# Routing of a mixture-of-experts stage, moved into the drain of the scan before it

## The reference, cut to what matters

```
h = layernorm(x) * (1 + ca) + sa
x = x + ga * scan_layer(h)            # in_proj, conv, selective scan, out_proj
h = layernorm(x) * (1 + cb) + sb      # [8192 tokens, 256]
s = h @ Wg                            # 8 logits a token
routed = softmax(s[:, :7]); keep only the largest, divided by itself
shared = softmax(s[:, 7:])            # one expert that every token passes
y = sum over experts e of gate_e * ((silu(h @ W1b_e) * (h @ W1a_e)) @ W2_e)
out = x + gb * y
```

## Time and profile before

| | us |
|---|---|
| median of 3 runs (lowest, highest) | 2514.27 (2513.76, 2518.05) |
| the profiled execution, its own time | 2508.63 |
| its span, first to last instruction | 2506.6 |
| PE busy in the span | 2176.9 (87%) |
| DVE busy | 1929.8 (77%) |
| POOL busy | 1955.7 (78%) |
| ACT busy | 1360.7 (54%) |

### The profile page before, as it was taken

The page is one execution under the profiler, slowest core; times in us unless marked ns, Lnnn a source line. Parts: engine busy times, 40 slices in busy tenths (PEclk is TensorE's granted clock), DMA queues, the critical chain, the costliest instruction groups (busy, mean ns, idle before and its releaser), DMA issues. The chain is left out here.

```text
span 2506.6 us, 31126 instructions
## 1 busy us (share of the span) xinstructions
PE 2176.9 (87%) x7664; PEld 1058.5 (42%) x7665; DVE 1929.8 (77%) x2060; ACT 1360.7 (54%) x2440; POOL 1955.7 (78%) x840
## 2 busy tenths in 40 slices
PE   8769898988989898999898898989857649999997
PEld 3214343443434343434343443434323335566654
DVE  2799999999999999989999999999897162222222
ACT  3666666667575766666666667576644232222221
POOL 1999889898989898988989898989897014555553
PEclk9868989898989898988989898989878869999999
DMA  5443242424232333424242424232321062222221
GB/s 154 135 110 94 76 103 67 101 68 113 81 92 74 96 82 87 116 79 105 68 103 69 101 68 111 81 94 77 89 68 42 24 208 76 85 84 83 87 85 45
DMA packets 149401, 224.39 MB, mean 90 GB/s; under 512 B 48227, under 2 KB 85617, under 8 KB 145138
## 3 DMA queue, kind: packets, MB, share of 16 engines
q1 hardware_dynamic: 135858, 182.44, 28.0%
q0 software_dynamic: 13376, 40.12, 5.2%
HBM read 99.48 MB, written 31.47 MB: 52 GB/s over the span
## 5 line engine op out<-in xcount | busy, mean ns | idle before, releaser
L1023 POOL TENSOR_TENSOR hs<-hs,c_rep 128x2048 f32<-128x2048 f32 x256 | 1154.5, 4528 | 37.3 <-ACT state L767 37.2
L863 DVE TENSOR_TENSOR_SCAN hs<-dA,state,hs 128x512 f32<-128x512 f32 x768 | 931.1, 1264 | 21.0 <-ACT dA L747 16.7
L747 ACT ACTIVATE dA<-d_rep,a 128x512 f32<-128x512 f32 x1024 | 690.0, 686 | 427.7 <-DVE hs L863 423.2
L1016 POOL TENSOR_TENSOR hs<-u_rep,b_rep 128x2048 f32<-128x2048 f32 x96 | 435.5, 4536 | 88.9 <-PE bank L517 88.9
L850 DVE TENSOR_TENSOR hs<-u_ps,b_rep 128x2048 f32<-128x2048 f32 x160 | 360.9, 2272 | 8.0 <-issue 4.8
L488 PE MATMUL bank<-n,w1s 128*128 128x512 f32 x512 | 268.4, 661 | 68.0 <-DVE delta L831 39.2
L863 DVE TENSOR_TENSOR_SCAN hs<-dA,hs 128x512 f32<-128x512 f32 x256 | 294.0, 1202 | 19.7 <-ACT dA L747 18.6
L517 PE MATMUL bank<-hs,spread 128*32 128x512 f32 x2048 | 280.3, 696 | 32.1 <-POOL hs L1023 28.0
L1408 DVE TENSOR_TENSOR hid<-z,sg 128x512 f32<-128x512 f32 x70 | 48.4, 692 | 298.1 <-ACT sg L1386 298.1
L1326 PE MATMUL z<-w1r,hT 128*128 x560 | 260.5, 608 | 3.4 <-issue 2.4
L446 PE MATMUL bank<-xin,w_in 128*128 128x512 f32 x512 | 245.1, 619 | 9.2 <-ACT xin L600 9.2
(11 more groups left out here) (173 smaller groups left out, 2531.9 us busy)
## 6 DMA issues: line engine op xcount, KB each, us to landing
d_rep<-delta SPq DMA_DIRECT2D x1024, 64.0 KB, 2.0
u_rep<-us SPq DMA_DIRECT2D x384, 64.0 KB, 2.0
b_rep<-bc_rows SPq DMA_DIRECT2D x64, 256.0 KB, 4.7
c_rep<-bc_rows SPq DMA_DIRECT2D x64, 256.0 KB, 7.8
xres<-in_x SPq DMA_DIRECT2D x16, 512.0 KB, 3.6
token_rows<-xpad SPq DMA_DIRECT2D x32, 256.0 KB, 2.3
token_rows<-xres SPq DMA_DIRECT2D x16, 512.0 KB, 3.0
xin<-in_x SPq DMA_DIRECT2D x15, 512.0 KB, 9.5
```

The lines of the kernel that those rows point to most:

```text
L747: nc.scalar.activation(dA[:, u % ABANK, :], d_rep[:, q, :], ACT.Exp, scale=t["a"][:, u:u + 1]).then_inc(da_ready, 1)
L863: nc.vector.tensor_tensor_scan(hs[:, s % RING, g, :], dA[:, u % ABANK, :], hs[:, s % RING, g, :], state[:, u:u + 1] if m else 0.0, ALU.mul ...
L1016: nc.gpsimd.tensor_tensor(hs[:, s % RING], u_rep[:, i % UBUF, :].unsqueeze(1).to_broadcast([P, NG, T]), b_rep[:, par, :].rearrange("p (g t ...
L1023: nc.gpsimd.tensor_tensor(hs[:, s % RING, :, :], hs[:, s % RING, :, :], c_rep[:, par, :].rearrange("p (g t) -> p g t", g=NG), ALU.mult).th ...
```

## The change

The routing program goes; its work moves into the drain of the fused program, in two parts, and its barrier goes with it. Part one (index 0) is tiles 0 to 59, whose logits are in memory when body 15 ends; part two (index 1) is the last chunk's four tiles, read from `lg` directly, whose logits are no longer stored. All tables live in memory that the drain no longer uses (`Room` hands it out: first weights, `us`, `delta`, spreads); sums and `placed` in PSUM banks of the scan.

Slot tiles are no longer sorted by expert. Each expert's running count starts at 127; where it crosses a multiple of 128 the next free slot tile goes to that expert (`allot`, `hand_out`), so tiles are numbered in order of arrival and part one's are final without knowing part two. `settle` computes each token's slot. The expert's number is packed above the token number (`pack`) and goes through the same matmul, from which `owner` is read at the end. The gate half of `sel`, ACT's before, and the number half, DVE's before, are now one POOL multiplication (`weigh_slots`), in groups with two alternating buffers. PE gets `count` and `place` between its items, and ACT two exponentials.

SP loads the expert weights during the drain, `w2r` as soon as the last scan products are made and `w1r` after the last `SUM`, into the memory of the scan's ring and of `b_rep` and `c_rep`, right behind the `XR` load. In the experts program the gate rows get a semaphore of their own, so that the first transposes wait for the token rows only, and in body 0 PE does `z` of tile 0 ahead of turning tile 1.

The core of the diff, shortened:

```diff
+            hold(sp, logits_stored, 16 * (NCHUNK - 1), held)
+            sp.dma_start(early_logits, logits_dram[0:EARLY_TILES * P]...).then_inc(early_loaded, 16)
+            def load_routed():
+                hold(sp, hc_ready, NSET * NCHUNK, held)
+                sp.wait_ge(dbu_own, N_OWN * NCHUNK)
+                sp.wait_ge(dbu_shared, N_SHARED * NCHUNK)
+                for e in range(NR):
+                    sp.dma_start(t["w2r"][:, e], ...).then_inc(w_routed, 16)
+                hold(sp, y_ready, KI * NCHUNK, held)
+                for e in range(NR):
+                    sp.dma_start(t["w1r"][:, e], ...).then_inc(w_routed, 16)
             for c in (NCHUNK, NCHUNK + 1):
                 for kind, n in transfers:
                     ...
                         transfer(kind, n, c, c % CPB)
+                        if kind == "XR":
+                            load_routed()
...
+            def count(i):
+                r = parts[i]
+                pe.wait_ge(onehot, i + 1)
+                if i == 0:
+                    pe.wait_ge(consts, 11)
+                nc.tensor.matmul(flat(r.total), ones, flat(r.one), start=True, stop=True).then_inc(counted, 1)
+                nc.tensor.matmul(flat(r.prefix), below, flat(r.one), start=True, stop=True).then_inc(counted, 1)
+            def place(g):
+                pe.wait_ge(id_ready, g + 1)
+                pe.wait_ge(lane_ready, g + 1)
+                for n, j in enumerate(groups[g]):
+                    last = nc.tensor.matmul(placed, at_lane[:, g % 2, n, :], sel[:, g % 2, n, :], ...)
+                last.then_inc(placed_made, 1)
+            PLACES = {("OP", 0): [(count, 0)], ("B", 2): [(count, 1)], ("A", 0): [(place, 0), (place, 1)], ("A", 1): [(place, 2)],
+                      ("A", 2): [(place, 3)], ("A", 3): [(place, 4)], ("Y", 0): [(place, 5), (place, 6)]}
...
+            route_exp(0)
             for item in [...]:
                     do(item, NCHUNK, 0)
+                    if item[0] == ("B", 0):
+                        route_exp(1)
...
+            def spread_slots(g):
+                dve.wait_ge(slots_known, 1 + g // len(EARLY_GROUPS))
+                if g >= 2:
+                    dve.wait_ge(placed_made, g - 1)
+                v.tensor_tensor(at_tile[:, g % 2, 0:n], among(kidx, SLOT_TILES), spread(r.tile, SLOT_TILES), ALU.is_equal).then_inc(at_ready, 1)
+                v.tensor_tensor(at_lane[:, g % 2, 0:n], among(lanes, P), spread(r.lane, P), ALU.is_equal).then_inc(lane_ready, 1)
+            FIRST, LAST = 0, 1
+            ROUTED = {("Y", 1): [(choose, FIRST)], ("SUM", 3): [(pick, FIRST)], ("OP", 0): [(allot, FIRST)],
+                      ("LN2", 0): [(hand_out, FIRST), (settle, FIRST), (weigh, FIRST), (spread_slots, 0), (soften, LAST), (spread_slots, 1),
+                                   (choose, LAST), (pick, LAST), (weigh, LAST), (allot, LAST), (hand_out, LAST), (settle, LAST)],
+                      ("A", 0): [(spread_slots, 2)], ("A", 1): [(spread_slots, 3)], ("A", 2): [(spread_slots, 4)],
+                      ("A", 3): [(spread_slots, 5), (spread_slots, 6)], ("Y", 0): [(spread_slots, 7)]}
+            soften(FIRST)
             for c in (NCHUNK, NCHUNK + 1):
                 ...
                         do(item, c, c % CPB)
+                        if c == NCHUNK:
+                            for step, n in ROUTED.get(item[0], []):
+                                step(n)
+            spread_slots(len(groups) - 1)
...
+            def weigh_slots(g):                                   # POOL, after its own last items
+                hold(pool, at_ready, g + 1, held)
+                if g >= 2:
+                    pool.wait_ge(placed_made, g - 1)
+                nc.gpsimd.tensor_tensor(sel[:, g % 2, 0:n]..., at_tile[:, g % 2, 0:n]..., r.value[:, first:first + n]..., ALU.mult).then_inc(id_ready, 1)
...
-                pe.wait_ge(fetched[q], 32 * n + 32)
+                pe.wait_ge(fetched[q], 16 * n + 16)
...
+                if first(k, 1):
+                    expert_in(k, q)
                 if not is_last(k, 1):
                     turn(*at(1))
                 if not first(k, 1):
                     turn_hid(*at(-1)[:2])
-                expert_in(k, q)
+                    expert_in(k, q)
```

More of the change, by code:

```diff
@@ L15 @@
+import math
 from contextlib import ExitStack
@@ L55 @@
 EMPTY = 1 << 20
+GR = 8
+EARLY_TILES = NTILE - TT
+EARLY_GROUPS = [range(g, min(g + GR, EARLY_TILES)) for g in range(0, EARLY_TILES, GR)]
+PACK = BATCH * SEQ * 2
 def hold(eng, sem, value, held):
@@ L62, in hold, with __init__, take @@
     eng.sem_inc(held, 1)
+class Room:
+    def __init__(self, *parts):
+        self.parts = [[part, 0] for part in parts]
+    def take(self, shape, dt=F32):
+        size = math.prod(shape)
+        for part in self.parts:
+            if part[1] + size <= part[0].shape[1]:
+                x = part[0][:, part[1]:part[1] + size]
+                part[1] += size
+                x = x if dt == F32 else x.bitcast(dt)
+                names = "abc"[:len(shape)]
+                return x.rearrange("p (" + " ".join(names) + ") -> p " + " ".join(names), **dict(zip(names, shape))) if len(shape) > 1 else x
+        raise ValueError("no room")
+class Routing:
+    def __init__(self, take, n, logits, keep_e, keep_w, total, prefix):
+        self.n, self.w, self.logits, self.keep_e, self.keep_w, self.total, self.prefix = n, n + 1, logits, keep_e, keep_w, total, prefix
+        self.ex, self.pr, self.mask, self.cum, self.work = (take([n, NR]) for _ in range(5))
+        self.one = take([NR, n])
+        self.tot, self.incl, self.nt, self.hd, self.nn, self.held = (take([NR, n + 1]) for _ in range(6))
+        self.ii = take([NR, n + 1], I32)
+        self.new, self.alloc = take([n, NR]), take([n, NR])
+        self.mx, self.rs, self.pm, self.ss, self.slot, self.tile, self.lane = (take([n]) for _ in range(7))
+        self.value = take([n, 2])
+        self.posi, self.lanei = take([n], I32), take([n], I32)
 def fused_program(nc, ins, t, bc_dram, wout_dram, w2_dram, mod_dram, gb_dram, rows_dram, logits_dram):
@@ L366, in transfer @@
                     store_rows(c - 1)
-                elif kind == "LOG":
+                elif kind == "LOG" and not (known(c) and c == NCHUNK):
                     store_logits(c - 1)
@@ L581, in _ @@
                         group(g, off, c, c % 2)
+                        if off == -1 and c == NCHUNK:
+                            for step, n in PLACES.get(g, []):
+                                step(n)
+            place(7)
+            pe.wait_ge(id_ready, len(groups))
+            pe.wait_ge(lane_ready, len(groups))
+            for n, j in enumerate(groups[-1]):
+                last = nc.tensor.matmul(placed, at_lane[:, (len(groups) - 1) % 2, n, :], sel[:, (len(groups) - 1) % 2, n, :], start=False, stop=(j == NTILE - 1))
+            last.then_inc(all_placed, 1)
         @block.scalar
@@ L1239, in experts_program @@
+            for g in range(len(groups)):
+                weigh_slots(g)
 def experts_program(nc, t, rows_dram, gb_dram, out):
@@ L1435, in build @@
             fused_program(nc, ins, t, bc_dram, wout_dram, w2_dram, mod_dram, gb_dram, rows_dram, logits_dram)
[L1436 to L1441 removed]
+        experts_program(nc, keep, rows_dram, gb_dram, out)
 def laid_out(x):
```

320 lines of the change are left out of this document (171 added, 149 removed).

## The result

The kernel after takes **2471.86 us** (median of 4 runs, 2468.68 to 2473.09) against 2514.02 for the kernel before in the same comparison (4 runs, 2513.11 to 2518.05). The ratio is 0.9827, 95% interval 0.981 to 0.9844. The direction was right, the size was not.

A forecast was written before the change was run, and what follows sets the result against it. PE bounds the routed experts, so whatever starts them earlier is gained whole: 27.5 us up to POOL's first copy plus 2.2 at the expert start, 29.7; 2478.9 plus 5.6 carried over gives 2484.6 us, range 2474 to 2494.

The forecast's parts named there:

- The weights are hidden: Drain: 11.0 MB of expert weights start at 1941 and are in by 1980.5, hidden by 40 us.
- rival B: Drain: the weight loads hold back `xres`, which `OP0` needs; 2489.5 us at half price, chance 0.10.
- Turns between DVE and POOL: Drain: POOL's `weigh_slots` holds part two's subtraction 2.4 us and `choose(1)`'s multiplication 2.2; `onehot` comes at 1978.2.
- The tail of routing: After the last accumulation: last spread, POOL, `place` and DVE steps take 5.8 us, then a barrier of 0.5.
- The expert start: Filling of the expert pipeline: first `z` 6.0 us behind POOL's first copy, second at 16.1 against 18.3; gain 2.2.
- rival D: Routed experts: slot tiles in arrival order change the expert at most tiles; at 0.5 us a tile 2519.6, chance 0.03.
- The 5.6 us carried from the profiled execution to the median: Whole kernel: median of runs 2514.27 lies 5.6 us above the profiled 2508.63; added to 2478.9.
- From `A0` to the last accumulation: End of drain: 28.5 us of PE work in one queue; 30.1 us from first read against 19.9 now, +10.2.
- The added wait on PE: Drain: `count(1)` waits 4.9 us for part two's `onehot`, with `B3` and `A0` queued behind; `A0` 7.7 later, clock included.
- the clock: Drain: PE's gap ahead of `count(1)` is followed by a granted clock of 0.50, +1.7 us.
- The normalisation: Drain: `count(0)` on PE makes `OP1` 0.65 us late, and the normalisation and all behind it 0.65 late.
- Rival A: Drain: no turns between DVE and POOL, no clock drop; gain 39.1 us, 2475.2, chance 0.18.

The follow-up runs named there:

- experiment 4: Kernel after with the expert weights loaded behind the drain, after SP's waits for `ACC` and `ROWS`: 2500.27 us, ratio 0.9957.
- experiment 3: Kernel after with POOL's first two `weigh_slots` held back until part two's slots are known: 2476.69 us, ratio 0.9860.
- experiment 2: Kernel after with the two edits in the experts program taken back: 2479.32 us, ratio 0.9868.
- experiment 11: Kernel before, unchanged, profiled once more: one run, 2514.66 us.
- experiment 1: Kernel before with only the experts program's two edits (gate rows' own semaphore, first `z` ahead of tile 1's transposes): 2504.56 us, ratio 0.9965.
- experiment 5: Kernel before with only the gate rows' own semaphore: one run, 2506.01 us.
- experiment 6: Kernel before with only the first `z` ahead of tile 1's transposes, gate and token rows on one semaphore: one run, 2518.53 us.
- experiment 9: Kernel before with DVE's wait on `fetched` written twice: one run, 2510.1 us.
- experiment 10: Kernel before with the gate rows' own semaphore, but PE waiting for both semaphores: one run, 2508.65 us.
- experiment 7: Kernel after with each `place` matmul of the first 60 tiles issued twice, the copy into unused PSUM: median 2477.15 us, ratio 0.9861.

## Why the prediction was wrong in size, step by step

Right:
- *The weights are hidden, at no cost* (experiment 4), and `xres` is not held back: in the kernel after `OP0` is read at 1951.91, straight after PE's result. That is rival B gone.
- *Turns between DVE and POOL*, from the one row: both appeared, at the two places named, and vanish in experiment 3. There were more places than forecast (below). The Trainium skill, "SBUF — State Buffer", section "Who interferes with whom", lets reductions through, which no row of before showed; here it agrees: the reduction at 1979.53 takes 0.17 beside POOL's multiplication, the two-input instruction 0.4 us later 1.63.
- *The tail of routing*: 6.4 from the last accumulation to the copy, forecast 6.2.
- *The expert start*: first `z` at 6.0 as forecast. The second at 15.8 against 16.1 is partly luck, since it moves by over 1 us with the clock.
- *The order of slot tiles costs nothing a tile* (rival D): 415.3 us over the tiles against 415.6, and 415.3 again in experiment 2, whose experts program is that of before.
- *The 5.6 us carried from the profiled execution to the median*: experiment 11 shows that execution to have had an early scan end.

Wrong, in the order of size:
- **The end of the kernel, 5.2 us, missing from the sum.** "Expert start" priced the semaphore split for the first tile only. Experiments 1, 2, 5, 6, 9 and 10 tie the 5.2 to it. Nothing in the profile before would have given this number; but the 12.0 us between the last store and the end were there to be asked about.
- **"From `A0` to the last accumulation", 30.1 forecast, 26.7 measured.** The bound was the one named (experiment 7); the size of its work was not. "28.5 us in one queue" added recorded durations: 3 x 2.0, 2 x 3.7, 7 x 2.15. Counted from start to start, as the profile after and experiment 7 show them, the same work is 3 x 1.71 + 2 x 3.45 + 7 x 1.91 = 25.4. Nor does that whole queue lie behind the first read: `place(0)` and `(1)` began at 1986.54, right behind `A0`'s multiplication and 3.1 us ahead of DVE's read. The forecast's steps from one read to the next were 4.2, 5.1, 4.4, 7.2 and 8.5; measured are 3.6, 4.8, 3.7, 6.5 and 7.3. In them lie three `A`, five `place` groups and two `Y`, so durations in place of distances make 3 x 0.29 + 5 x 0.24 + 2 x 0.25 = 2.6 of the 3.4; the other 0.8 are not split further. The profile before had the distance for `B`, the shape of `A`: ACT's copies of it begin 1.71 us apart (1971.30, 1973.01, 1974.73).
- **"The added wait on PE" and "the clock", 2.6 us together.** `count(1)` waited 1.04 instead of 4.9, and no clock drop followed. `onehot(1)` came at +45.1 (forecast +46.6): the turns cost 3.1 instead of 4.6, because POOL's multiplication needs 2.0 us alone (two took 4.08 in experiment 3), not 2.57, which I had scaled from another shape. And PE's `B2` ended at +44.1, 2.5 later than in before instead of 0.65, so that the gap shrank from the other side too (2.1 of it is the next point; and the clock was 0.50 in the first 3.65 us of `B`, where before had 0.65). The first `A` was read at +52.2 (forecast +54.8), and now DVE's own list set it: it ends 0.8 behind SiLU. The forecast's own terms, 1984.4 + 1.7, give 1986.1 or +54.5: it had put the clock's 1.7 on top of DVE's list (1984.7), which doesn't wait for `B3`.
- **The normalisation was 2.1 late, not 0.65.** 0.8 is the read of `OP1`, and only half of that was forecast: `count(0)` cost 0.4 (forecast 0.65), while the other 0.4 looks like a third turn. DVE's subtraction of part one took 3.68 us instead of 0.60 because POOL's last scan product ran until 1942.32, so `Y1`, done by PE at 1942.33, was read only at 1942.69; the forecast had "nothing" for it. 1.3 was not seen either: POOL's two small steps of the reciprocal root took 0.75 us beside DVE's scan of `hand_out` (which ends at 1960.64) and 0.93 beside the instruction behind it (1961.59), each ending as DVE's does, and the step behind them 0.1 more. All this is read from the rows; no run takes it away. In the timeline of POOL before they were these:

```profile
1953.34 0.23 POOL L994 TENSOR_SCALAR mv<-mv 128x4 f32<-128x4 f32 x1 [16.79 <-DVE mv L824]
1953.66 0.23 POOL L995 TENSOR_SCALAR mv<-mv 128x4 f32<-128x4 f32 x1
```

  The forecast asked only whom POOL delays, not whom DVE delays. It made PE's `B2` later, but not the first `A`, for which DVE's own list was last.

Rival A ("no turns", 2475.2) lies nearest to the time, but it is refuted: its mechanism was not there, and its time was nearly met, by luck, through other gains. The range was too narrow because it held only errors of the terms that I had listed.

## What to carry to other kernels

Add up the work of a full queue from start to start of its instructions; recorded durations in an unbroken row overlap, and their sum was 12% too long here (28.5 against 25.4; a single `place` matmul has 0.40 recorded and 0.24 apart). Where an instruction is moved off a loaded stretch, look at what its consumer has left to do when it lands: twice here POOL's work, taken out of DVE's way, left PE empty for more than what DVE had won. And compare two profiles from an anchor behind the part that the change doesn't touch, since that part alone moved by up to 9 us between executions.

## What the runs showed of the hardware that was not expected

- A semaphore of its own for one of two transfers, used in a loop of 70 tiles, shortens the end of the kernel by 5.2 us in every profile that has it (tail 17.3 in nine, 22.5 or 22.6 in the five without). A further wait on the same semaphore does not. The cause is open.
- DVE and POOL delay each other both ways: 128x28 on DVE went from 0.19 to 1.84 us behind a POOL multiplication, and 128x420 from 0.60 to 3.68; 128x4 on POOL went from 0.23 to 0.75 beside a DVE scan and to 0.93 beside a `scalar_tensor_tensor`, both with two inputs in SBUF.
- Empty stretches of PE of 1.0 and 1.7 us (ahead of `count(1)` and of `place(2)` in the kernel after) left the granted clock at 1.00; empty stretches of 3.2 and 4.3 us were followed by slower rows (2.91 for a `place` that takes 2.07, at a mean granted 0.74; and 6.77 for two, at 0.50 over the first 3.2).
- The end of an unchanged scan of 1930 us lay between 1931.6 and 1940.9 in the profiles, while drain and routing behind it repeated within 0.1.
